# Attention scores and value products in one 64-row by 32-column tiling of the TensorE array, side results in the score slots

## The chip, the cores and the metric

One core of one Trainium2 chip runs the whole kernel. The metric is the device time of one execution in microseconds (us). Engines are named as in the profile: PE (TensorE, matmuls) and PEld (its weight loads), DVE (VectorE), ACT (ScalarE), POOL (GpSimd), SP (SyncE, which issues the DMAs). PSUM, where matmuls put their results, is used as eight banks of 128 partitions by 512 fp32 values, numbered 0 to 7.

## The reference

A block of three residual steps on x of 4096 tokens by 256 features. In short:

```python
x = x + 0.5 * ffn(layernorm(x))          # base 256x256, a shared and six routed rank-16 adapters, top 2 of 6
x = x + attn(layernorm(x))
x = x + 0.5 * ffn(layernorm(x))          # the same weights

def attn(x):                              # 16 heads of 16 features, T = 4096
    q, k, v = x @ Wq.T, x @ Wk.T, x @ Wv.T
    q, k = layernorm_per_head(q) * 256**-0.25, layernorm_per_head(k) * 256**-0.25
    dot = q @ k.T                         # per head, causal: j > i masked
    return (softmax(dot) @ v).reshape(T, 256) @ Wo.T + bo
```

## The kernel before

**Tiling.** Tokens are cut into 8 chunks of 512 queries (`CH`), heads into 4 groups of 4. For each chunk and group the keys are walked in blocks of 128. The work is counted in *units* (`attention_units`): a unit is 1024 columns of scores, two banks of PSUM, in full blocks two heads by 512 queries against one key block. Two units make a *batch* (one key block, four heads; one of the diagonal batches is a single unit). Chunk c has 20 + 32c units, 1056 in all, so chunks 1 to 7 have 52, 84, 116, 148, 180, 212 and 244.

**Stages of a unit.** `scores(u)` (L1356): for each of two heads a matmul of keys (50 rows: two fp16 parts of the head, their cross terms and two rows of shift; 128 key columns) by queries (512 columns, fp16), the two heads in the upper and lower 64 rows of the array and in the two banks of slot `u % 3` (`SLOTS = 3`: banks 0 to 5). `exp` (L776) on ACT reads the two banks at once, 1024 columns, and writes one of five places of the ring of probabilities (fp32). `mask` (L724) on POOL zeroes what lies above the diagonal. `values(b)` (L1374) takes a batch: for each of four heads a matmul of the 128 keys' values (17 columns: 16 features and a column of ones, which gives the softmax's sum) by the probabilities (128 rows, 512 columns, fp32), the four heads in four column strips of 32 and all in bank 6 (`ACC`). An fp32 matmul shows as two MATMUL records, so a full batch has eight. After a group's last batch DVE transposes bank 6 into SBUF (`gather`, L1159) and divides by the sum (`divide`, L1164, L1166).

**Side work.** Everything else (layernorms, the two FFNs of other chunks, q/k/v of the next chunk, the output projection of the one before) is cut into stages that are mixed into the attention of each chunk: `turn`, `turnin` and `heads` (four fp32 transposes each on PE), `qk` (6 matmuls of 512 columns), `value` and `projout` (12 of 256), `inner` (24 of 118), `outer` (18 of 256). Each such piece writes one bank, number 7 (`SIDE`), while attention runs, and DVE (for some stages of the first chunks ACT) reads it out. `turn` and `turnin` are read twice: a copy to fp16 (L846) and the remainder (L848).

**Order.** All engines follow one list, `ORDER` (`schedule`, L230). In step u it has: `exp` u, `mask` u, side stages of place 3u, `scores` u+2, `divide` where due, side stages of place 3u+1, `values` of a batch that ended at unit u-1 (u-2 if masked), side stages of place 3u+2. The table `PLACES` gives the place of each side stage within its chunk. Each engine executes its part of the list strictly in this order, waiting on semaphores. `Pass.__init__` walks the list once to find, for each stage that writes a side bank, which bank it gets and whom it must wait for (`bank`, `last`, `done`). Scores of unit u wait for `exp` of u-3, values for `exp` (or `mask`) of the batch's last unit.

Of the kernel before, what the change touches and what calls it, by code (L numbers as in the profile page):

```python
# [41 lines left out]
ACC, SIDE = 6, 7  # L42
START_BANKS = (7, 5, 4, 3)
END_BANKS = (7, 0, 1, 2, 3, 4, 5)
# [176 lines left out]
def schedule():  # L221
# [28 lines left out]
    for u in range(NU):  # L250
# [8 lines left out]
        if BATCHES[b][2][-1] == u:  # L259
            values.append((u + (2 if BATCHES[b][3] else 1), b))  # L260
# [13 lines left out]
    for _, b in values:  # L274
        yield "values", b
        if b in GROUP_END:
            yield "gather", GROUP_END[b]
            groups.append((NU, GROUP_END[b]))
# [55 lines left out]
class Pass:  # L334
# [5 lines left out]
    def __init__(self, name, semaphore, order, banks, scalar, x, x_in, fronts, free=None):  # L340
# [16 lines left out]
        self.use, self.bank, self.done, self.last, self.scalar, self.high = {}, {}, {}, {}, scalar, {}  # L357
        held, count, rotate = {}, {self.read: 0, self.read_act: 0}, True
        for stage, n in order:
            rotate = rotate and stage != "scores"  # L360
            if free and (stage, n) == ("exp", NU - 1):

                rotate, banks = True, END_BANKS
                held.update({b: free for b in END_BANKS if b != SIDE})
# [16 lines left out]
def build(nc, ap, out, always_general=False):  # L381
    ctx = ExitStack()
    with ctx:
# [93 lines left out]
        def bank(b, n=1):  # L477
# [14 lines left out]
        s_ok, exp_ok, mask_ok, pv, acc_read, bo_ok, att_ok = (semaphore(q) for q in (  # L492
            "s_ok", "exp_ok", "mask_ok", "pv", "acc_read", "bo_ok", "att_ok"))
# [8 lines left out]
        main = Pass("m", semaphore, ORDER, START_BANKS, on_scalar, x_main, lambda c: (x_in[c], 16), 2, (exp_ok, NU))  # L502
# [226 lines left out]
        def _(act):  # L729
# [25 lines left out]
            for stage, n in ORDER:  # L755
# [15 lines left out]
                elif stage == "exp":  # L771
# [4 lines left out]
                    act.activation(probs[:, u % RING, :], bank(2 * (u % SLOTS), 2), ACTF.Exp, bias=0.0, scale=1.0).then_inc(exp_ok, 1)  # L776

        @block.vector
        def _(dve):
# [324 lines left out]
            dve.memset(bank(ACC), 0.0).then_inc(zeroed, 1)  # L1104
# [44 lines left out]
            for stage, n in ORDER:  # L1149
                front_and_heads(main, stage, n)  # L1150
                if stage == "gather":
# [7 lines left out]
                    dve.transpose(oT[:, :], bank(ACC)).then_inc(acc_read, 1)  # L1159
                elif stage == "divide":  # L1160
# [5 lines left out]
                    dve.tensor_tensor(att[:, g // 2, :, g % 2 * HS:(g % 2 + 1) * HS], turned[:, :, 0:HS],  # L1166
# [282 lines left out]
```

## Time and profile before

| | |
|---|---|
| runs shown | 1196.37, 1195.91, 1195.37 us; median 1195.91 |
| span of the profiled execution | 1192.3 us, 3.6 us below that median (start and end of the program lie outside it) |
| PE busy | 1104.1 us, 93% |
| ACT busy | 1014.7 us, 85% |
| DVE, POOL busy | 467.5 and 241.6 us, 39% and 20% |
| first and last `exp` | about 96 and 1159 us from the start of the span |
| chain that ended last | PE 72%, ACT 13%, issue 6%, DVE 6% |

The page's busy time of PE is from the first column sent to the end of the last matmul as modelled; matmuls overlap, in different strips of the array above all, so a busy PE is not one at its peak. A timeline row gives the start of a group of like instructions, the time from its first start to its last end, their number, and in brackets how long the engine had been idle.

### The profile page before, as it was taken

To read this page: it belongs to the slowest core of one execution; us is meant where nothing else is said; L and a number is where in the kernel's file an instruction comes from. 1 tells how busy PE (TensorE), PEld (TensorE's weight loads), DVE (VectorE), ACT (ScalarE), POOL (GpSimd) and SP (SyncE) were. 2 spreads that over 40 slices of the span, in tenths; PEclk is the share of its full clock that TensorE was granted. 3 is DMA by queue.
4 is the path that set the end of the run, shared out by engine and by line. 5 is a ranking of instruction groups with operands and counts; after the bars stand their busy time and mean duration, and the time that the engine had idled before them with its cause. 6 is when DMAs were issued, how large, how long until landed. Compare 5 with 4: busy or idle time off the path is not lost.

```text
span 1192.3 us, 22761 instructions
## 1 busy us (share of the span) xinstructions
PE 1104.1 (93%) x8884; PEld 359.6 (30%) x8884; DVE 467.5 (39%) x1181; ACT 1014.7 (85%) x1134; POOL 241.6 (20%) x377
## 2 busy tenths in 40 slices
PE   3758999999999999999999999999999999999994
PEld 3534333332323233232332232232222222222123
DVE  5678665554544353333333323423131222021114
ACT  3216788789888998999999999999999999999980
POOL 2236533222122211212022021012110101010100
PEclk9779999999999999999999999999999999999996
DMA  5022202003000300003000022000001100000000
GB/s 145 3 63 60 59 11 81 1 28 99 1 1 19 93 17 1 1 32 92 4 1 1 1 67 60 1 1 2 1 10 48 53 1 1 10 10 1 1 19 18
DMA packets 39608, 33.37 MB, mean 28 GB/s; under 512 B 8722, under 2 KB 39432, under 8 KB 39496
## 3 DMA queue, kind: packets, MB, share of 16 engines
q1 hardware_dynamic: 37364, 31.74, 9.0%
q8 instruction: 73, 1.20, 0.4%
q10 hardware_dynamic: 2132, 0.12, 0.1%
q14 instruction: 39, 0.32, 0.1%
HBM read 18.73 MB, written 12.85 MB: 26 GB/s over the span
## 4 chain that ended last, share of the span: by engine, by line
PE 72%; ACT 13%; issue 6%; DVE 6%; DMA 1%; POOL 1%; SPq 0%; ACTq 0%; DVEq 0%; POOLq 0%
PE ps L1190 68%; ACT ring L776 13%; PE ps L1232 2%; PE ps L1298 1%; DMA x<-in_x 1%; DVE st L807 1%; PE ps L1252 1%; DVE area L828 1%; DVE oT L1159 0%; POOL rstd L711 0%; POOL sq L532 0%; DVE x L980 0%; DVE ss L985 0%; DVE sq L1013 0%; ACT area L765 0%
## 5 line engine op out<-in xcount | busy, mean ns | idle before, releaser
L776 ACT ACTIVATE ring<-ps 128x1024 f32<-128x1024 f32 x1056 | 982.2, 1115 | 65.5 <-PE ps L1190 63.5
L1190 PE MATMUL ps<-ring,vf 128*17 128x512 f32 (+3 forms) x4608 | 559.4, 562 | 5.0 <-DVE oT L1159 4.4
L1190 PE MATMUL ps<-queries,keys 50*128 50x512 f16 (+3 forms) x2304 | 363.2, 366 | 22.1 <-ACT ring L776 4.9
L1190 PEld LDWEIGHTS ps<-queries,keys 50*128 50x128 f16 x2304 | 92.3, 93 | 475.3 <-ACT ring L776 437.3
L724 POOL TENSOR_SCALAR_AFFINE_SELECT ring<-ring 128x256 f32<-128x256 f32 (+1 forms) x224 | 103.9, 481 | 396.5 <-ACT ring L776 392.6
L1190 PEld LDWEIGHTS ps<-ring,vf 128*17 128x17 f32 x4608 | 79.7, 95 | 174.5 <-issue 144.2
L711 POOL TENSOR_TENSOR rstd<-var,minus_half 128x4 f32<-128x4 f32 x24 | 24.4, 1017 | 235.6 <-DVE var L813 235.4
L980 DVE SCALAR_TENSOR_TENSOR x<-ps,power,x 128x512 f32<-128x512 f32 x32 | 24.0, 750 | 110.7 <-PE ps L1190 110.7
L846 DVE CAST xnT<-ps 128x512 f16<-128x512 f32 x32 | 22.1, 691 | 100.0 <-PE ps L1232 100.0
L1190 PE MATMUL ps<-baseT,xnT 128*128 128x256 f16 x384 | 55.0, 283 | 3.9 <-DVE area L848 3.8
L1232 PE MATMUL ps<-ident,area 128*128 128x128 f32 x192 | 34.2, 311 | 20.0 <-DVE area L828 20.0
L765 ACT ACTIVATE xnT<-ps 128x512 f16<-128x512 f32 x16 | 9.6, 599 | 49.9 <-PE ps L1232 49.9
L1159 DVE STREAM_TRANSPOSE oT<-ps 128x512 f32<-128x512 f32 x32 | 22.9, 715 | 71.0 <-PE ps L1190 70.5
L1190 PE MATMUL ps<-qkT,xnT 128*128 128x512 f16 x192 | 48.7, 394 | 1.7 <-DVE xnT L848 1.5
L532 POOL TENSOR_TENSOR sq<-area 128x512 f32<-128x512 f32 x32 | 33.5, 1047 | 67.2 <-DVE ss L985 41.7
L1190 PEld LDWEIGHTS ps<-baseT,xnT 128*128 128x128 f16 x384 | 36.7, 101 | 19.2 <-issue 11.0
L828 DVE TENSOR_SCALAR area<-x,mv,rstd 128x256 f32<-128x256 f32 x96 | 36.9, 444 | 11.3 <-POOL rstd L711 11.3
L1013 DVE TENSOR_SCALAR sq<-ps,scaled 128x512 f32<-128x512 f32 x16 | 12.9, 806 | 70.1 <-PE ps L1298 70.1
L537 POOL TENSOR_TENSOR split<-sq,split 128x512 f16<-128x512 f32 x16 | 18.8, 1175 | 100.0 <-DVE split L1017 100.0
L807 DVE BATCH_NORM_STATS2 st<-x 128x6 f32<-128x256 f32 x96 | 33.5, 412 | 9.5 <-DMA x<-in_x 4.8
L1232 PEld LDWEIGHTS ps<-ident,area 128*128 128x128 f32 x192 | 23.6, 156 | 43.0 <-issue 36.9
L848 DVE TENSOR_TENSOR xnT<-ps,xnT 128x512 f16<-128x512 f32 x48 | 33.1, 691 | 7.6 <-ACT xnT L765 6.3
(153 smaller groups left out, 670.5 us busy)
## 6 DMA issues: line engine op xcount, KB each, us to landing
parts_d<-split SPq DMA_DIRECT2D x32, 256.0 KB, 2.6
keys<-parts_d SPq DMA_DIRECT2D x96, 64.0 KB, 2.3
queries<-parts_d SPq DMA_DIRECT2D x192, 32.0 KB
x<-in_x SPq DMA_DIRECT2D x8, 512.0 KB, 4.2
out_x<-x SPq DMA_DIRECT2D x16, 256.0 KB, 2.2
queries<-shift_d SPq DMA_DIRECT2D x64, 4.0 KB
ring<-in_base_W SPq DMA_DIRECT2D x1, 256.0 KB, 4.9
ring<-in_Wq SPq DMA_DIRECT2D x1, 256.0 KB, 3.8
```

Of the source, the lines that this page charges most:

```text
L532: e.tensor_tensor(sq[:, :], qn[:, n % TC, :], qn[:, n % TC, :], ALU.mult).then_inc(K.sq_ok, 1)
L711: pool.tensor_tensor(rstd[ln][:, :], var[ln][:, 0, :], minus_half[:, :].broadcast_to([P, TC]), ALU.pow).then_inc(main.rstd_ok[ln], 1)
L724: m = pool.affine_select(out=tiles[:, part, :], in_=tiles[:, part, :], compare_op=ALU.is_ge, fill=0.0, base=0, pattern=[[0, len(range(8)[p ...
L776: act.activation(probs[:, u % RING, :], bank(2 * (u % SLOTS), 2), ACTF.Exp, bias=0.0, scale=1.0).then_inc(exp_ok, 1)
L807: dve.bn_stats(st[ln][:, i, :], x[:, i, :]).then_inc(*own.up())
L828: m = dve.tensor_scalar(xn[ln][:, i, :], x[:, i, :], mv[ln][:, i, 0:1], rstd[ln][:, i:i + 1], ALU.subtract, ALU.mult)
L846: dve.tensor_copy(high, src).then_inc(*K.own.up())
L848: dve.tensor_tensor(low, src, high, ALU.subtract).then_inc(K.read, 1)
L980: dve.scalar_tensor_tensor(out=x, in0=bank(K.bank[key]).rearrange("p (n d) -> p n d", n=2), scalar=power[0][:, 5:6], in1=x, op0=ALU.mult, ...
L1159: dve.transpose(oT[:, :], bank(ACC)).then_inc(acc_read, 1)
L1190: return pe.matmul(o, lhsT, rhs, start=start, stop=stop, skip_group_check=True)
L1232: m = pe.transpose(b[:, ib * D + i * P:ib * D + (i + 1) * P], xn[ln][:, 2 * a + i, ib * P:(ib + 1) * P], ident[:, :])
```

## The change

Three things, all in one diff.

1. **One tiling.** A score matmul of 50x128 keys becomes four of 50x32 (32 keys each), so a unit is 8 matmuls of 512 columns in the 8 tiles of 64 rows by 32 columns. A value matmul is cut by rows: 64 keys each, upper and lower half. The accumulator is now two banks, 6 and 7 (`ACC`), one for the even and one for the odd 128-query tiles of the chunk. A batch's values come in two parts. In part 0 the upper rows work on one bank and the lower rows on the other; in part 1 they swap. Each part of a full batch is 8 matmuls of 256 columns (16 MATMUL records). Part 1 waits for the semaphore `pv_first` that part 0 raises.
2. **Order.** Part 0 stands in the step of the batch's last unit (one step earlier than the values before), part 1 in the next step.
3. **Side results.** Bank 7 is gone as a side bank. A side piece takes a bank of one of the three score slots: the planner in `Pass.__init__` gives it the slot that comes free first, counts the slot as taken for `SIDE_UNITS` = 2.2 units, and lets a second piece within a step share it. Scores take the slot that comes free first, and wait for whoever used it, an `exp` or a side reader. `gather` transposes two banks of 256 columns, `divide` has two multiplications.

```diff
-ACC, SIDE = 6, 7
+ACC = 6, 7
+SIDE = 7
...
+SIDE_UNITS = 2.2
...
-            values.append((u + (2 if BATCHES[b][3] else 1), b))
+            values += [(u + (2 if BATCHES[b][3] else 0) + part, (b, part)) for part in range(2)]
...
-        while values and values[0][0] <= u:
-            b = values.pop(0)[1]
-            yield "values", b
-            if b in GROUP_END:
+        first = False
+        while values and values[0][0] <= u and not first:
+            b, part = values.pop(0)[1]
+            first = part == 0
+            yield "values", (b, part)
+            if part == 1 and b in GROUP_END:
...
+            elif stage == "scores":
+                s = min(range(SLOTS), key=lambda q: (free[q], q))
+                free[s], shared[s] = n + 1, -2
+                self.slot[n], self.slot_free[n] = s, sorted({held[b] for b in (2 * s, 2 * s + 1) if b in held}, key=lambda q: (q[0].name, q[1]))
+                held[2 * s] = held[2 * s + 1] = (exp_ok, n + 1)
             if stage in BANK_STAGES:
                 i = len(self.use)
-                b = banks[i % len(banks)] if rotate else SIDE
+                if rotate:
+                    b = banks[i % len(banks)]
+                else:
+                    s = min(range(SLOTS), key=lambda q: (shared[q] < now - 1, free[q], q))
+                    b = 2 * s + (last_side + 1) % 2 if shared[s] >= now - 1 else 2 * s
+                    free[s], shared[s], last_side = now + SIDE_UNITS, now, b
...
-                    act.activation(probs[:, u % RING, :], bank(2 * (u % SLOTS), 2), ACTF.Exp, bias=0.0, scale=1.0).then_inc(exp_ok, 1)
+                    act.activation(probs[:, u % RING, :], bank(2 * main.slot[u], 2), ACTF.Exp, bias=0.0, scale=1.0).then_inc(exp_ok, 1)
...
-                    dve.transpose(oT[:, :], bank(ACC)).then_inc(acc_read, 1)
+                    for i in range(2):
+                        m = dve.transpose(oT[:, i * CH // 2:(i + 1) * CH // 2], bank(ACC[i])[:, 0:CH // 2])
+                    m.then_inc(acc_read, 1)
...
-                if u >= SLOTS:
-                    pe.wait_ge(exp_ok, u - SLOTS + 1)
+                for key in main.slot_free[u]:
+                    pe.wait_ge(*key)
...
+                for pair in zip(blocks[0::2], blocks[1::2]):
+                    for k in range(0, P, 32):
+                        for h, j, q0, w, b, col in pair:
+                            half = slice(HR * (h % 2), HR * (h % 2) + SH + 2)
+                            m = mm(bank(2 * main.slot[u] + b)[k:k + 32, col:col + w], keys[half, h // 2, j * P + k:j * P + k + 32],
+                                   queries[half, h // 2, q0:q0 + w], True, True)
...
+                    pe.wait_ge(pv_first, b + 1)
+                runs = [], []
+                for h, j, q0, w, bk, col, u in [block + (u,) for u in units for block in UNITS[u][2]]:
+                    for rows in range(2):
+                        i = (b + part + rows) % 2
+                        tiles = [q for q in range(q0 // P, (q0 + w) // P) if q % 2 == i]
...
+                            runs[rows].append((h % GH, bank(ACC[i])[32 * (h % GH):32 * (h % GH) + VL, tiles[0] // 2 * P:(tiles[-1] // 2 + 1) * P],
+                                               vf[HALF * rows:HALF * (rows + 1), j, HEAD[h], :], moving))
+                for pair in itertools.zip_longest(*(sorted(runs[rows], key=lambda q: q[0]) for rows in range(2))):
+                    for run in pair:
+                        if run:
+                            m = mm(*run[1:], first and part == 0, last and part == 1)
+                m.then_inc((pv_first, pv)[part], 1)
```

How PE's instructions move, at a `turn` in chunk 6 (a piece of four transposes, `ps<-ident,area`). `ps<-queries,keys` are scores, `ps<-ring,vf` are values; the semaphores waited for stand in brackets (`m_read` is raised by DVE's reads of side banks, `exp_ok` by ACT's exponentials). PE before:

```order
L1190 MATMUL ps<-queries,keys 128x512 [waits exp_ok]
L1190 MATMUL ps<-queries,keys 128x512
L1232 MATMUL ps<-ident,area 128x128 [waits m_xn_ok0,const,m_read]
L1232 MATMUL ps<-ident,area 128x128 x3
L1190 MATMUL ps<-queries,keys 128x512 [waits exp_ok]
L1190 MATMUL ps<-queries,keys 128x512
L1190 MATMUL ps<-ring,vf 17x512 [waits exp_ok]
L1190 MATMUL ps<-ring,vf 17x512 x3
L1190 MATMUL ps<-queries,keys 128x512 [waits exp_ok]
L1190 MATMUL ps<-queries,keys 128x512
```

The same piece on PE after the change (L1214 and L1256 are the helpers L1190 and L1232):

```order
L1214 MATMUL ps<-ring,vf 17x256 [waits exp_ok]
L1214 MATMUL ps<-ring,vf 17x256 x7
L1256 MATMUL ps<-ident,area 128x128 [waits m_xn_ok0,const,exp_ok]
L1256 MATMUL ps<-ident,area 128x128 x3
L1214 MATMUL ps<-queries,keys 32x512 [waits exp_ok]
L1214 MATMUL ps<-queries,keys 32x512 x7
L1214 MATMUL ps<-ring,vf 17x256 [waits pv_first]
L1214 MATMUL ps<-ring,vf 17x256 x7
L1214 MATMUL ps<-queries,keys 32x512 [waits m_read,exp_ok]
L1214 MATMUL ps<-queries,keys 32x512 x7
```

The piece now waits for an exponential instead of the last reader of bank 7, the first values stand ahead of the next scores instead of behind them, and the second scores behind the piece wait for DVE's reads of it.

## Rows read from the trace of the kernel before

**Rows 1.** The page: busy time by engine; chain that ended last.
```profile
PE 1104.1 (93%) x8884; PEld 359.6 (30%) x8884; DVE 467.5 (39%) x1181; ACT 1014.7 (85%) x1134; POOL 241.6 (20%) x377
PE 72%; ACT 13%; issue 6%; DVE 6%; DMA 1%; POOL 1%; SPq 0%; ACTq 0%; DVEq 0%; POOLq 0%
```

**Rows 2.** Busy time by stretch, chunks 2, 3, 6, 7; length, engines, PEclk (granted clock), DMA.
```profile
190.00:282.00 92.00, 90.82 (x770) 30.72 (x762) 47.69 (x108) 78.84 (x86) 26.90 (x41) 1.00 0.14 42
282.00:404.00 122.00, 120.50 (x1012) 39.02 (x1008) 59.40 (x146) 108.69 (x119) 29.85 (x45) 1.00 0.10 28
...
727.00:930.00 203.00, 199.26 (x1590) 54.52 (x1586) 59.50 (x144) 197.08 (x216) 28.61 (x43) 1.00 0.04 13
930.00:1159.00 229.00, 218.31 (x1706) 54.21 (x1702) 38.14 (x96) 224.82 (x247) 18.98 (x35) 1.00 0.04 10
```

**Rows 3.** Chain of waits, 950 to 970 us, in order of time: start, length, what.
```profile
950.47 1.09 ACT ring L776
951.55 0.05 issue
951.60 8.16 PE ps L1190 x62
```

**Rows 4.** Timeline, 950 to 952 us: start, length, engine, instruction.
```profile
950.09 0.13 PEld L1190 LDWEIGHTS ps<-ring,vf 128*17 128x17 f32 x8 [0.23 <-issue]
950.09 1.05 PE L1190 MATMUL ps<-ring,vf 128*17 128x512 f32 x8
951.07 0.92 PE L1190 MATMUL ps<-queries,keys 50*128 50x512 f16 x4
```

**Rows 5.** Timeline, 839 to 843 us: a `qk` piece and what follows.
```profile
839.14 1.47 PE L1190 MATMUL ps<-qkT,xnT 128*128 128x512 f16 x6
840.54 0.39 PE L1190 MATMUL ps<-queries,keys 50*128 50x512 f16 x2
840.86 1.05 PE L1190 MATMUL ps<-ring,vf 128*17 128x512 f32 x8
841.85 0.61 PE L1190 MATMUL ps<-queries,keys 50*128 50x512 f16 x4
842.34 2.85 ACT L776 ACTIVATE ring<-ps 128x1024 f32<-128x1024 f32 x3 [0.28 <-PE ps L1190]
842.38 1.05 PE L1190 MATMUL ps<-ring,vf 128*17 128x512 f32 x8
```

**Rows 6.** Timeline of PE, 91 to 93.5 us, before attention begins.
```profile
91.22 0.60 PE L1232 MATMUL ps<-ident,area 128*128 128x128 f32 x4
91.66 1.46 PE L1190 MATMUL ps<-qkT,xnT 128*128 128x512 f16 x6
92.95 0.60 PE L1232 MATMUL ps<-ident,area 128*128 128x128 f32 x4
```

**Rows 7.** Timeline, 871 to 876 us: an `outer` piece.
```profile
871.53 0.83 PE L1190 MATMUL ps<-baseT,xnT 128*128 128x256 f16 x6
...
873.61 0.39 PE L1190 MATMUL ps<-queries,keys 50*128 50x512 f16 x2
...
874.10 1.02 ACT L776 ACTIVATE ring<-ps 128x1024 f32<-128x1024 f32 x1 [0.59 <-PE ps L1190]
```

**Rows 8.** Timeline, 751 to 757 us: a `turn` piece.
```profile
751.15 9.27 ACT L776 ACTIVATE ring<-ps 128x1024 f32<-128x1024 f32 x10
...
754.77 0.66 PE L1232 MATMUL ps<-ident,area 128*128 128x128 f32 x4
755.36 0.39 PE L1190 MATMUL ps<-queries,keys 50*128 50x512 f16 x2
755.46 0.69 DVE L846 CAST xnT<-ps 128x512 f16<-128x512 f32 x1 [4.79 <-PE ps L1232]
...
756.19 0.69 DVE L848 TENSOR_TENSOR xnT<-ps,xnT 128x512 f16<-128x512 f32 x1
```

**Rows 9.** Groups of instructions by line and shape: count, busy us, mean ns.
```profile
L776 ACT ACTIVATE ring<-ps 128x1024 f32<-128x1024 f32 x1056 | 982.2, 1115 | 65.5 <-PE ps L1190 63.5
...
L1190 PEld LDWEIGHTS ps<-ring,vf 128*17 128x17 f32 x4608 | 79.7, 95 | 174.5 <-issue 144.2
```

More of the change, by code:

```diff
@@ L273, in schedule @@
         yield from beside(3 * u + 2)
-    for _, b in values:
-        yield "values", b
-        if b in GROUP_END:
+    for _, (b, part) in values:
+        yield "values", (b, part)
+        if part == 1 and b in GROUP_END:
             yield "gather", GROUP_END[b]
@@ L334, with __init__ @@
 class Pass:
-    def __init__(self, name, semaphore, order, banks, scalar, x, x_in, fronts, free=None):
+    def __init__(self, name, semaphore, order, banks, scalar, x, x_in, fronts, exp_ok=None):
         def s(q):
@@ L1368, in scores @@
                         pe.wait_ge(main.k_in[c][g // 2], 6 * 16)
-                for h, j, q0, w, b, col in blocks:
-                    half = slice(HR * (h % 2), HR * (h % 2) + SH + 2)
-                    m = mm(bank(2 * (u % SLOTS) + b)[:, col:col + w], keys[half, h // 2, j * P:(j + 1) * P],
-                           queries[half, h // 2, q0:q0 + w], True, True)
+                for pair in zip(blocks[0::2], blocks[1::2]):
[4 more added lines that the diff above has]
+                                   queries[half, h // 2, q0:q0 + w], True, True)
@@ L1373, in scores, with values @@
                 m.then_inc(s_ok, 1)
-            def values(b):
+            def values(b, part):
                 c, g, units, masked, first, last = BATCHES[b]
-                if first and b >= 1:
-                    pe.wait_ge(acc_read, NG * c + g)
-                elif first:
-                    pe.wait_ge(zeroed, 1)
-                if first and g == 0:
-                    for a in range(2):
-                        pe.wait_ge(*main.done["value", (c, a)])
-                if masked:
-                    pe.wait_ge(mask_ok, MASKED[units[-1]])
-                else:
-                    pe.wait_ge(exp_ok, units[-1] + 1)
-                blocks = sorted([(q0, h % GH, h, j, w, u, bk, col) for u in units for h, j, q0, w, bk, col in UNITS[u][2]])
-                for q0, k, h, j, w, u, bk, col in blocks:
-                    m = mm(bank(ACC)[32 * k:32 * k + VL, q0:q0 + w], vf[:, j, HEAD[h], :], probs[:, u % RING, bk * CH + col:bk * CH + col + w], first, last)
-                m.then_inc(pv, 1)
@@ L1394, in _ @@
-            before = [q for q in ORDER[:ORDER.index(("scores", 0))] if q[0] in BANK_STAGES]
-            side_last = [main.done[[q for q in before if main.bank[q] == b][-1]] for b in START_BANKS[1:]]
+                if part == 0:
+                    if first and b >= 1:
+                        pe.wait_ge(acc_read, NG * c + g)
+                    elif first:
+                        pe.wait_ge(zeroed, 1)
+                        pe.wait_ge(*main.acc_free)
+                    if first and g == 0:
+                        for a in range(2):
+                            pe.wait_ge(*main.done["value", (c, a)])
+                    if masked:
+                        pe.wait_ge(mask_ok, MASKED[units[-1]])
+                    else:
+                        pe.wait_ge(exp_ok, units[-1] + 1)
+                else:
+                    pe.wait_ge(pv_first, b + 1)
@@ L1400, in _ @@
                 elif stage == "values":
-                    values(n)
+                    values(*n)
                 elif stage == "projout":
```

39 lines of the change are left out of this document (26 added, 13 removed).

## The prediction

> **What bounds the kernel now.** I read the page first, then the stretches, then single timelines. On the page PE is the busiest engine and the chain that ended last lies on it for 72%, on ACT for 13% [rows 1]. The stretches say that this is no one bound. A run of undisturbed `exp` (ten in 9.27 us, the last lasting 1.115) starts one every (9.27 - 1.115) / 9 = 0.906 us [rows 8, 9]. By that pace the units of chunks 2, 3, 6 and 7 would take 76.1, 105.1, 192.1 and 221.1 us. Their stretches took 92, 122, 203 and 229 [rows 2]. ACT therefore lost 15.9, 16.9, 10.9 and 7.9 us there: ACT is the floor, and PE sometimes comes late. About 1063 us of the span are attention, against 1056 x 0.906 = 957 for the exponentials alone.
>
> **What PE pays for a change of tiling.** Six `qk` matmuls take 1.29 us where four fp32 transposes of the same 128x128 tiling follow (91.66 to 92.95), and the transposes 0.44 each time [rows 6]; going from fp32 to fp16 costs nothing. Where scores follow, the same six take 839.14 to 840.54, 1.40 us [rows 5]. The number format is the same there and the tiling changes: 0.11 us a switch. Scores to values and back cost that too: values take 0.99 us (840.86 to 841.85), two units of scores 0.53 (841.85 to 842.38) [rows 5], a batch 1.52. Without the two switches it is 1.30: scores 0.21 a unit, values 0.44 a half. The Trainium skill (TensorEngine Tiling (Array Packing), Key Properties) says that changing the tiling mode drains TensorE; by that rule, the trace agrees.
>
> **The time PE has.** An `exp` starts 0.49 us after the first matmul of its scores when ACT is waiting (873.61 to 874.10, 841.85 to 842.34) [rows 5, 7]. PE continues 0.05 after an `exp` has ended [rows 3], that is 1.16 after its start. So scores released by the `exp` three units back have 3 x 0.906 - 1.16 - 0.49 = 1.07 us until ACT stalls. Let time 0 be PE's release by the last `exp` of a batch, step E; the step after it is O.
>
> Before: O's scores start at 0, values 0.32 to 1.31, the next E's scores at 1.31 (limit 0.906 + 1.07 = 1.98), PE idle from 1.63 to 1.81. A side piece may be 0.67 long without a stall if it stands behind O's scores, or at place 0 of E, and 0.85 if it stands in front of O's scores, using the idle 0.18. I test this on the trace. Long pieces last, with their switch, 1.40 (`qk`), 2.08 (`outer`, 871.53 to 873.61 [rows 7]), and by 0.11 a matmul of 256 columns about 1.42 (`value`, `projout`) and 1.32 (`inner`), 22.2 us in a full chunk. In chunk 6, 13 of its 14 have 0.85 and one 0.67: 22.2 - 11.7 = 10.5 against 10.9 found. In chunk 7 eight have 0.85: 13.8 - 6.8 = 7.0 against 7.9. Chunks 2 and 3 give 9.2 and 12.5 against 15.9 and 16.9: there pieces stand 4 units apart and PE does not recover between them (chunk 3: 58 x 1.52 + 29.3 of side pieces = 117 of 122 us).
>
> **After, term by term.** The order is now: values part 0 at 0 to 0.44, O's scores at 0.44 (limit 1.07), part 1 to 1.09, next E's scores at 1.09 (limit 1.98), idle from 1.30 to 1.81. The idle time grows from 0.18 to 0.51, but:
> - A piece now pays two switches, one more (0.11), and eight tiles start one after another. Eight weight loads of 0.095 fit in 0.13 [rows 4, 9], some 0.005 apart, so I take 0.04 for the last of eight.
> - A piece at place 1 asks for the slot of the running `exp` and waits for its end: it can't use the idle time. Behind it come a half of values, then scores. It has 1.07 - 0.44 = 0.63 (E), 1.98 - 0.906 - 0.44 = 0.63 (O).
> - At place 2 of E or place 0 of O it has 0.63, at place 2 of O or place 0 of E 1.98 - 1.09 = 0.89.
>
> Less 0.15 for the first point, the room is 0.48 or 0.74. Counted in the order, 90 long pieces: 36 go from 0.85 to 0.48 (+0.37 each), 17 from 0.67 to 0.48 (+0.19), 37 from 0.67 to 0.74 (-0.07): 13.3 + 3.2 - 2.6 = **+13.9 us**. Short pieces last 0.59 (754.77 to 755.36 [rows 8]) and stall nothing now; 32 of them will be 0.11 over: **+3**.
>
> Then the side readers. Bank 7 made nobody wait but the next side piece; now 140 units of scores wait for a reader, usually four units after the piece. A `turn` is read out 2.11 after its start (754.77 to 756.19 + 0.69) [rows 8], 2.2 with release and switch, against a limit of 1.98 after its slot was released. At place 1 (14 pieces read twice) that is 0.2 late, at place 2 of O (11, started 0.18 later) 0.4, of E (5, 0.44 later) 0.65: 10 us, less what is counted above, **+8.5** if DVE is free at once. Pieces at place 0 start a unit earlier and are in time; single reads of 0.7 behind long pieces stay inside the stall that the piece has made.
>
> What dense chunks get back: PE's need in chunk 3 falls from 117 to 58 x 1.30 + 29.3 + 26 x 0.11 = 107.6, some 4 more for part 1's wait on part 0 (0.07 each, when only one unit of scores lies between), against ACT's 105. The 4.4 and 6.7 us lost there beyond the single pieces (chunks 3, 2) should shrink by more than half, and chunks 0, 1 and 4 give some: **-10**, between 0 and -15. The tail: part 1 waits for part 0 with nothing between, two transposes for one, two multiplications: **+0.5**. `gather`, `divide` and the unbalanced parts of one diagonal batch in each group (32 x 0.2 us of PE) lie beside ACT otherwise.
>
> Sum: 13.9 + 3 + 8.5 - 10 + 0.5 = 15.9 on the span of 1192.3; with the 3.6 outside it, **1211 us**. PE's work falls by 528 x 0.22 - 167 x 0.11 = 98 us (167 side pieces, 90 long and 77 short), and the time does not follow, since ACT sets the pace and the slots are fewer.
>
> **The eight tiles.** No row shows fp32 in both row halves at once, and none eight tiles. Bounds: full overlap, as in the four strips [rows 4] and the two score halves, or a load that isn't hidden. In the trace eight loads run under the first four matmuls in the same rows (950.09), so I take full overlap. The Trainium skill (TensorE: Matmul & The Clock Gate, The mechanism) says that LDWEIGHTS overlaps in-flight matmuls only when the row group differs; here the trace disagrees. It is a rival below.
>
> **Rivals.**
> - *Faster: the relief of PE wins.* If rooms stay as they are (scores caught up by the 0.51 idle time, DVE quick), only the dense term is left: 1196 - 10 = 1186, at best some 1178. For: PE is on 72% of the chain. Against: the room counted above decides, not PE's sum; it turns where the mean room of long pieces exceeds today's 0.75. Chance 0.27.
> - *Nothing to measure:* terms cancel within 0.2%, 2.4 us, which is what a measurement here can tell. 0.08.
> - *Slower by my sum:* 1211 (1199 to 1222). 0.42.
> - *Readers are late.* DVE works in order and is busy a third to a half of the time [rows 2]; behind a read stand operations of 0.4 to 0.8 us or a wait for another engine, and scores, hence ACT, wait for it. Another 0.2 at each of 140 units: about +25, 1236. 0.16.
> - *Loads or row halves don't overlap.* If each wave of eight (six in a batch) pays a load of 0.095, a batch is 1.87 and everything is bound by PE: 528 x 1.87 and about 90 x 1.6 + 77 x 0.59 of side pieces make 1177 in place of 1063, 1310 us. It decides from 0.5 us more a batch. 0.07.
>
> **Numbers.** The likeliest is 1211. The range 1186 to 1236 takes in the bounds of the dense and the reader's term and half of the faster case. Faster 0.27, same 0.08, slower 0.65.
>
> **What would show it.** Right: no step of 0.1 between scores and values, a batch's matmuls 1.3 apart where PE is behind, PE idle more, and more than 11 and 8 us lost by ACT in chunks 6 and 7, less than 16 and 17 in chunks 2 and 3. Scores four units behind a `turn` would be released by DVE's second read of it. Wrong: stalls behind single long pieces in chunk 6 no longer than now (the rooms were miscounted); a gap left at scores to values (the switch was not the tiling); or starts of eight matmuls spread by more than 0.1 us (the tiles don't overlap).

## The result and the profile after

The changed kernel takes 1309.4 us (median of 4 runs, 1307.11 to 1312.3), beside 1196.03 for the kernel before on the same chip: ratio 1.095, 95% interval 1.0932 to 1.0969. It is slower by 113 us. The forecast had the sign, 15 us and a range that ended at 1236. One rival names 1310 us; it met the number by chance, since what it says of the hardware is not what the traces below show.

The page of the changed kernel, the rows that answer to [rows 1] and the first of [rows 9]:

```profile
PE 1125.3 (86%) x29108; PEld 558.9 (43%) x29108; DVE 480.6 (37%) x1245; ACT 1024.6 (78%) x1134; POOL 237.3 (18%) x377
...
PE 42%; ACT 24%; issue 19%; DVE 11%; DMA 1%; SPq 1%; POOL 1%; DVEq 0%; ACTq 0%; POOLq 0%
...
L794 ACT ACTIVATE ring<-ps 128x1024 f32<-128x1024 f32 x1056 | 991.7, 1066 | 159.8 <-PE ps L1214 156.0
```

One `exp` lasts less than before (1066 ns against 1115), yet ACT is idle 160 us in front of its exponentials where it was 65.5. PE's share of the last chain falls from 72% to 42%, and DVE's rises from 6% to 11%: more of the time is waiting from engine to engine. The same four stretches as [rows 2], chunks 2, 3, 6 and 7:

```profile
217.00:324.00 107.00, 95.44 (x2447) 48.02 (x2442) 48.76 (x117) 80.16 (x86) 27.14 (x41) 0.98 0.12 35
324.00:459.00 135.00, 122.72 (x3264) 62.35 (x3256) 63.13 (x153) 109.91 (x120) 29.25 (x45) 1.00 0.10 27
810.00:1031.00 221.00, 200.41 (x5564) 92.02 (x5544) 60.33 (x152) 199.30 (x216) 28.27 (x43) 1.00 0.06 15
1031.00:1271.00 240.00, 217.69 (x6256) 94.09 (x6240) 39.51 (x104) 226.02 (x247) 17.95 (x35) 1.00 0.05 13
```

Against the pace of 0.906 us a unit, ACT now loses 30.9, 29.9, 28.9 and 18.9 us there, where it lost 15.9, 16.9, 10.9 and 7.9. Nothing came back in the dense chunks.

**Does the tiling work?** A plain stretch of the changed kernel's timeline in chunk 6:

```profile
1000.02 0.66 PE L1214 MATMUL ps<-ring,vf 64*17 64x256 f32 x16 [0.16 <-ACT ring L794]
1000.25 0.14 PEld L1214 LDWEIGHTS ps<-queries,keys 50*32 50x32 f16 x8
1000.46 0.43 PE L1214 MATMUL ps<-queries,keys 50*32 50x512 f16 x8
1000.80 0.16 PEld L1214 LDWEIGHTS ps<-ring,vf 64*17 64x17 f32 x16 [0.40 <-PE ps L1214]
1000.80 0.65 PE L1214 MATMUL ps<-ring,vf 64*17 64x256 f32 x16
1001.24 0.43 PE L1214 MATMUL ps<-queries,keys 50*32 50x512 f16 x8
1001.86 0.65 PE L1214 MATMUL ps<-ring,vf 64*17 64x256 f32 x16 [0.18 <-ACT ring L794]
```

It does. A part (16 records) holds PE for 0.44 us, from 1000.02 to 1000.46, as forecast for a half without switches; the next scores follow at once, and their eight weights were loaded 0.2 us earlier under running matmuls. The next batch begins 1.84 later, about ACT's pace for two units (1.81), and PE waits for ACT there. The one flaw is small: part 1 starts 0.78 after part 0 and not 0.66, as it waits for part 0's last matmul to end.

**Where ACT loses time.** For the other comparisons I counted over each trace how much later than 0.906 us after the last one each `exp` starts. *Start of a group* means a masked unit or one of the four behind it, *full* everything else; delays under 0.03 are left out. *Scores*: the `exp` starts within 0.16 us of its scores' end. *Ring*: its scores were ready and it waited for something else. That is the place in the ring, or another instruction of ACT's own just ahead of it (a read of a side result, or the router's): at group starts 15 of the 31 us before are of the second kind and 16 of the 111 after, so the ring proper went from 16 to 95.

| us lost, all chunks | full, scores | full, ring | start, scores | start, ring | sum |
|---|---|---|---|---|---|
| before | 49 | 3 | 22 | 31 | 106 |
| after | 75 | 10 | 24 | 111 | 220 |

So 33 of the 114 us are in full stretches, and 81 at the starts of groups, a place to which the prediction gave no time of ACT's, only some of PE's.

**A bare start of a group**, with no side piece near it (first units 600 and 601, chunk 6, changed kernel, timeline):

```profile
813.08 4.14 ACT L794 ACTIVATE ring<-ps 128x1024 f32<-128x1024 f32 x4
...
814.31 0.41 PE L1214 MATMUL ps<-queries,keys 50*32 50x512 f16 x8
814.53 0.62 PE L1214 MATMUL ps<-ring,vf 64*17 64x256 f32 x16
815.23 0.41 PE L1214 MATMUL ps<-queries,keys 50*32 50x512 f16 x8
...
817.57 1.02 ACT L794 ACTIVATE ring<-ps 128x1024 f32<-128x1024 f32 x1 [0.35 <-PE ps L1214]
```

The ring has five places: `exp` u waits on `pv` until *all* values of the batch of unit u-5 are done (`pv` is raised by part 1 alone). Part 1 of units 600 and 601 starts at 814.53 and ends at 815.15; `exp` 605, whose scores were ready, starts at 815.28, 0.40 us late (the four exponentials from 813.08 take 4.14 us, at the pace 3 x 0.906 + 1.07 = 3.79). `exp` 607 at 817.57 is 0.46 late in the same way. Masked values stood two steps after their batch before the change; now part 0 stands there and part 1 a step later still. This start costs 0.87 us; it cost 0.03.

**The same place with a side piece**, units 706 to 711 of the changed kernel, timeline:

```profile
924.12 1.47 PE L1214 MATMUL ps<-qkT,xnT 128*128 128x512 f16 x6 [0.29 <-ACT ring L794]
...
925.52 0.41 PE L1214 MATMUL ps<-queries,keys 50*32 50x256 f16 x16
...
926.16 0.24 DVE L1184 RECIPROCAL den<-oT 128x16 f32<-128x16 f32 x1
926.43 0.64 DVE L1189 TENSOR_TENSOR att<-oT,den 128x128 f32<-128x128 f32 x2
927.00 0.68 DVE L854 COPY area<-ps 128x512 f32<-128x512 f32 x1
...
927.83 0.41 PE L1214 MATMUL ps<-queries,keys 50*32 50x512 f16 x8 [1.89 <-DVE area L854]
928.04 0.63 PE L1214 MATMUL ps<-ring,vf 64*17 64x256 f32 x16
...
929.56 1.94 ACT L794 ACTIVATE ring<-ps 128x1024 f32<-128x1024 f32 x2 [2.47 <-PE ps L1214]
```

The `qk` result is complete at 925.6, but DVE still has the router's work, the division and then the copy: it is read out at 927.68. The second scores behind the piece want that slot, so PE stands for 1.89 us, with the overdue values queued behind it, and ACT is idle for 2.47 us: first without scores (until 928.2), then without a place in the ring (until the values end at 929.47). This start loses 3.53 us, against 0.35 before.

Two theories stand against each other for the 98 us that the forecast missed. **Ring**: masked values a step later use up the five places. **Readers**: scores wait for DVE's read of a side bank. A third, **tiling**, would have the half batches and their order themselves cost more than they free.

### The profile page after: what moved, and what is told of

It reads as the page before. It is cut to its first block, busy times and chain, and to the rows that moved or that the text cites. A ratio compares the mean times of both kernels' runs of the same rounds, so it can differ in the third digit from the quotient of the medians.

```text
span 1305.4 us, 63412 instructions
## 1 busy us (share of the span) xinstructions
PE 1125.3 (86%) x29108; PEld 558.9 (43%) x29108; DVE 480.6 (37%) x1245; ACT 1024.6 (78%) x1134; POOL 237.3 (18%) x377
## 4 chain that ended last, share of the span: by engine, by line
PE 42%; ACT 24%; issue 19%; DVE 11%; DMA 1%; SPq 1%; POOL 1%; DVEq 0%; ACTq 0%; POOLq 0%
PE ps L1214 39%; ACT ring L794 24%; PE ps L1256 2%; DVE st L825 1%; DMA x<-in_x 1%; PE ps L1322 1%; DVE area L846 1%; DVE oT L1178 1%; DVE xnT L866 1%; DVE x L998 1%; DVE xnT L864 1%; SPq L616 1%; DVE att L1189 1%; SPq L604 1%; PE ps L1276 0%
## 5 line engine op out<-in xcount | busy, mean ns | idle before, releaser
L794 ACT ACTIVATE ring<-ps 128x1024 f32<-128x1024 f32 x1056 | 991.7, 1066 | 159.8 <-PE ps L1214 156.0
L1214 PE MATMUL ps<-ring,vf 64*17 64x256 f32 (+1 forms) x17920 | 696.4, 369 | 36.1 <-ACT ring L794 27.2
L1214 PE MATMUL ps<-queries,keys 50*32 50x512 f16 (+2 forms) x9216 | 448.5, 363 | 81.0 <-ACT ring L794 47.4
L1214 PEld LDWEIGHTS ps<-ring,vf 64*17 64x17 f32 x17920 | 240.0, 93 | 331.6 <-ACT ring L794 140.4
L1214 PEld LDWEIGHTS ps<-queries,keys 50*32 50x32 f16 x9216 | 150.7, 92 | 246.0 <-ACT ring L794 137.5
L742 POOL TENSOR_SCALAR_AFFINE_SELECT ring<-ring 128x256 f32<-128x256 f32 (+1 forms) x224 | 99.8, 461 | 434.1 <-ACT ring L794 431.3
L1214 PE MATMUL ps<-baseT,xnT 128*128 128x256 f16 x384 | 56.8, 289 | 4.8 <-DVE area L866 3.6
L1178 DVE STREAM_TRANSPOSE oT<-ps 128x256 f32<-128x256 f32 x64 | 24.9, 427 | 75.1 <-PE ps L1214 74.5
L1256 PE MATMUL ps<-ident,area 128*128 128x128 f32 x192 | 34.7, 315 | 20.2 <-DVE area L846 19.7
L1214 PE MATMUL ps<-qkT,xnT 128*128 128x512 f16 x192 | 48.5, 393 | 2.2 <-DVE xnT L866 1.5
L1214 PEld LDWEIGHTS ps<-baseT,xnT 128*128 128x128 f16 x384 | 37.3, 103 | 20.5 <-issue 8.7
L1256 PEld LDWEIGHTS ps<-ident,area 128*128 128x128 f32 x192 | 23.9, 157 | 37.9 <-issue 30.0
L854 DVE COPY area<-ps 128x512 f32<-128x512 f32 x20 | 13.8, 688 | 67.8 <-PE ps L1214 67.7
L825 DVE BATCH_NORM_STATS2 st<-x 128x6 f32<-128x256 f32 x96 | 33.5, 412 | 11.5 <-DMA x<-in_x 7.0
```

The costliest lines, as they stand in the source:

```text
L742: m = pool.affine_select(out=tiles[:, part, :], in_=tiles[:, part, :], compare_op=ALU.is_ge, fill=0.0, base=0, pattern=[[0, len(range(8)[p ...
L794: act.activation(probs[:, u % RING, :], bank(2 * main.slot[u], 2), ACTF.Exp, bias=0.0, scale=1.0).then_inc(exp_ok, 1)
L825: dve.bn_stats(st[ln][:, i, :], x[:, i, :]).then_inc(*own.up())
L1178: m = dve.transpose(oT[:, i * CH // 2:(i + 1) * CH // 2], bank(ACC[i])[:, 0:CH // 2])
L1214: return pe.matmul(o, lhsT, rhs, start=start, stop=stop, skip_group_check=True)
L1256: m = pe.transpose(b[:, ib * D + i * P:ib * D + (i + 1) * P], xn[ln][:, 2 * a + i, ib * P:(ib + 1) * P], ident[:, :])
```

## The experiments

In each, the ratio is to the kernel before on the same chip (its medians were 1193.6 to 1195.2). "From after" and "from before" say which kernel was edited.

### One cause at a time

**a_mask1**, from after: masked values one step earlier.

```diff
-            values += [(u + (2 if BATCHES[b][3] else 0) + part, (b, part)) for part in range(2)]
+            values += [(u + (1 if BATCHES[b][3] else 0) + part, (b, part)) for part in range(2)]
```

> The changed kernel, with both parts of a masked batch's values one step earlier (the second part where all of it stood before the change). Theory 'ring': exp u waits for the values of u-5 in the five-place ring, and the second part came one step later than the values did, so at the 28 diagonal group starts of chunks 1 to 7 exp stands waiting for values. Then the time falls from 1309 to 1235 to 1285 us, and the two stalls of 0.4 us in a bare group start (units 605 and 607) go. Rival 'slots': the stalls at group starts come from scores and side pieces that wait for a slot's reader, with the values queued behind them; then under 10 us come back. The earlier part may wait up to 0.5 us on POOL's mask, behind nothing that ACT needs at once.

1274.62 us, 1.0665 (1.0641 to 1.069): 35 us of the 113 come back by one digit. At the same bare start of a group ACT now runs through unit 605; 607 is still 0.48 us late, where the expectation had both stalls gone:

```profile
788.72 3.93 ACT L794 ACTIVATE ring<-ps 128x1024 f32<-128x1024 f32 x4
...
790.78 0.60 PE L1214 MATMUL ps<-ring,vf 64*17 64x256 f32 x13 [0.42 <-POOL ring L742]
...
792.81 2.85 ACT L794 ACTIVATE ring<-ps 128x1024 f32<-128x1024 f32 x3 [0.17 <-PE ps L1214]
```

Part 0 of units 602 and 603 now waits 0.42 us for POOL's mask, and part 1, for which `exp` 607 waits, stands behind it: the earlier place has a price too. The loss by the ring at group starts falls from 111 to 69 us (the ring proper from 95 to 42); by scores it rises from 24 to 32.

**a_order**, from after: both parts where the values stood before the change.

```diff
-            values += [(u + (2 if BATCHES[b][3] else 0) + part, (b, part)) for part in range(2)]
+            values += [(u + (2 if BATCHES[b][3] else 1), (b, part)) for part in range(2)]
-        while values and values[0][0] <= u and not first:
+        while values and values[0][0] <= u:
```

> The changed kernel, with both parts of a batch's values together in the step where the values stood before. Theory 'ring': the second part is again as early as before in masked batches, so the group starts lose 25 to 60 us less; in full batches part 1 waits about 0.3 us for part 0 with nothing between, the next scores start at 1.42 instead of 1.09 us and long pieces have some 0.4 instead of 0.48 us of room: 5 to 10 us more. In sum 1250 to 1290. Rival 'slots': no gain at group starts, 1310 to 1325.

1350.5 us, 1.1317 (1.1287 to 1.1348), above what either theory allowed and, with a_two below, the slowest here. Group starts lose 125 us, 10 less than in the changed kernel, but full stretches 133 instead of 85. The timeline shows why:

```profile
1000.57 0.64 PE L1212 MATMUL ps<-queries,keys 50*32 50x512 f16 x16
1001.00 1.42 PE L1212 MATMUL ps<-ring,vf 64*17 64x256 f32 x32
1002.22 0.64 PE L1212 MATMUL ps<-queries,keys 50*32 50x512 f16 x16
```

A batch takes 1.65 us, against 1.52 before: with nothing between the parts, values hold PE 1.22 (1001.00 to 1002.22) and not 0.88. Part 1 waits for part 0, and those 0.34 us are more than the two switches (0.22) cost. Splitting the batch over two steps is no ornament: the tiling needs it.

**b_slots**, from before: tiling and order untouched, side results put in score slots by the change's planner; bank 7 stays empty.

```diff
-                b = banks[i % len(banks)] if rotate else SIDE
+                else:
+                    s = min(range(SLOTS), key=lambda q: (shared[q] < now - 1, free[q], q))
+                    b = 2 * s + (last_side + 1) % 2 if shared[s] >= now - 1 else 2 * s
+                    free[s], shared[s], last_side = now + SIDE_UNITS, now, b
```

> The kernel before in its old tiling and order, with side results in the three score slots by the planner of the change (bank 7 idle in attention). By the rooms of the prediction: 36 long pieces from 0.85 to 0.67 (+6.5 us), 17 behind O's scores from 0.67 to 0.08, since they wait for the running exp (+10), readers late +10 to +20: 1220 to 1235. If slots cost nothing by themselves: 1196. If they are the whole loss: near 1309.

1277.97 us, 1.0696 (1.0675 to 1.0717), in none of the three forecasts: the slots cost 83 us by themselves, on average half a microsecond for each of 167 pieces. A `turn` of this kernel, timeline:

```profile
882.03 0.66 PE L1246 MATMUL ps<-ident,area 128*128 128x128 f32 x4
882.61 0.39 PE L1204 MATMUL ps<-queries,keys 50*128 50x512 f16 x2
882.72 0.69 DVE L860 CAST xnT<-ps 128x512 f16<-128x512 f32 x1 [6.29 <-PE ps L1246]
883.44 0.69 DVE L862 TENSOR_TENSOR xnT<-ps,xnT 128x512 f16<-128x512 f32 x1
884.28 0.39 PE L1204 MATMUL ps<-queries,keys 50*128 50x512 f16 x2 [1.28 <-DVE xnT L862]
...
884.77 1.02 ACT L790 ACTIVATE ring<-ps 128x1024 f32<-128x1024 f32 x1 [0.43 <-PE ps L1204]
```

Scores start 2.25 us after the start of the piece, right after DVE's second read, though DVE was free at once; `exp` is 0.43 late. The length of that wait was forecast (2.2), how often it counts was not. The longest of PE's waits from 100 to 1150 us in this kernel (in all, times, longest):

```profile
PE ps L1204 <- ACT ring L790: 32.8, 62, 1.6
PE ps L1204 <- DVE xnT L862: 13.2, 18, 1.3
PE ps L1204 <- DVE x L994: 6.0, 8, 1.7
PE ps L1204 <- DVE area L850: 5.7, 5, 1.9
PE ps L1204 <- DVE area L862: 4.2, 5, 1.3
PE ps L1204 <- DVE x L1198: 3.3, 5, 0.7
```

and the same list of the kernel before, where only two waits of 0.4 and 0.2 us in all follow:

```profile
PE ps L1190 <- ACT ring L776: 4.9, 12, 0.5
PE ps L1190 <- DVE oT L1159: 4.4, 3, 3.1
PE ps L1298 <- DVE area L1002: 1.6, 1, 1.6
```

Readers of side results are hardly in the second; in the first the five groups of them cost PE 32 us. PE's waits for `exp` grow by nearly as much (4.9 to 32.8): while a piece has a slot, scores must take one that a later `exp` still holds. The wait for readers and the wait for `exp` are both prices of sharing. This run doesn't separate them; a_side3 below trades one for the other.

**b_ring4**, from before: one place of the ring fewer, memory as it was.

```diff
-RING = 5
+RING = 4
```

> The kernel before with a ring of four places of probabilities in use instead of five. Theory 'ring': the ring is the limit at masked batches; with four places exp n of the first unit behind a masked batch comes 0.75 us late, twice or three times at each of 28 group starts, and full batches lose their slack behind pieces: 1250 to 1300, with ACT's waits at group starts. Rival: values are never what ACT waits for, under 1205.

1260.41 us, 1.0548 (1.0527 to 1.057). Time lost by the ring goes from 34 to 151 us, by scores from 72 to 20. The ring had no place to spare before the change; a step of delay is not free anywhere. (Six places weren't tried.)

### Which pieces pay for the slots

Three kernels from b_slots give bank 7 back to one class of pieces each, b_slots_g, b_slots_t and b_slots_l in this order. The condition stands ahead of the planner's choice:

```diff
+                elif any(UNITS[v][3] is not None for v in range(max(0, now - 2), min(NU, now + 3))):
+                elif stage in SPLIT_STAGES:
+                elif stage in ('qk', 'value', 'projout', 'inner0', 'inner1', 'outer0', 'outer1'):
+                    b = SIDE
```

> b_slots (1278 us), but the 55 side pieces that stand within two steps of a masked unit use bank 7 as before the change. Theory 'group starts': in b_slots exp lost 91 us there against 53 before, so 30 to 45 of the 83 us come back: 1233 to 1248. Rival 'everywhere alike': 55 of 167 pieces, 27 us: 1248 to 1255.

> b_slots, but the 49 pieces that DVE reads twice (turn, turnin) use bank 7. Theory 'readers': a turn alone in a full stretch costs 0.3 to 1.0 us in b_slots and nothing before, long pieces only 0.0 to 0.6 more than before: 49 x 0.65 = 32 us come back, 1240 to 1252. Rival 'running exp': the pieces' own wait for the running exp and the scores that wait two exps back are what costs, whatever the reader: 49 of 167, 24 us, 1252 to 1258.

> b_slots, but the 90 long pieces use bank 7; only the 77 short ones are in slots. Theory 'readers': shorts carry most of the cost: 18 to 30 us come back, 1248 to 1260. Rival 'running exp': long pieces carry it, since they can't use PE's idle time: 50 us or more come back, under 1230.

| bank 7 has | us | ratio (95%) | gained on b_slots | per piece |
|---|---|---|---|---|
| 55 near masked units | 1244.07 | 1.0422 (1.0396 to 1.0448) | 34 | 0.62 |
| 49 read twice | 1245.83 | 1.0425 (1.0397 to 1.0454) | 32 | 0.66 |
| 90 long | 1237.01 | 1.0351 (1.0325 to 1.0376) | 41 | 0.45 |

The first two came out as the theory in front had it, the third between its theory and its rival. No class is innocent. The first also says where group starts lose: with bank 7 there, the ring's loss at group starts is 33 us, beside 59 in b_slots and 31 before. With the long ones in bank 7, the 77 short ones still cost 43 us, 0.56 each. The forecast had 11.5 us for the short ones (3 and 8.5), and for the long ones their smaller rooms but nothing for their reader.

**a_side3**, from after: the planner counts a slot as taken a unit longer, so that scores come to it later.

```diff
-SIDE_UNITS = 2.2
+SIDE_UNITS = 3.2
```

> The changed kernel with the planner counting a slot as taken by a side piece for 3.2 units instead of 2.2: 355 instead of 226 units of scores wait for the exp two back, and readers have a unit more. Theory 'readers late are the cost': 20 us or more come back, under 1290. Theory 'the lost room is the cost' (scores with 0.16 us): 1310 to 1330.

1289.25 us, 1.0794 (1.0773 to 1.0815), 20 us better. By the order, 143 units of scores wait for a reader, as in the changed kernel, but further behind the piece; the price is that 355 instead of 226 scores must wait for the `exp` two units back. From 100 to 1150 us PE's waits for readers of side results fall from some 27 to 7 us (those for L866 from 6.0 us in 11 waits to 0.2 in one). The ring's loss at group starts hardly moves, 107 us for 111: what comes back lies in full stretches (85 to 70 us) and, at 7 us, at group starts.

### What the tiling itself does

Two score slots instead of three, and a fixed bank for side results that nobody else uses: no reader can hold scores up, and PE has little room, so its work should show.

```diff
-SLOTS = 3
+SLOTS = 2
```

That is all of **b_two** (from before, side bank 7). **a_two** (from after) has side results in bank 5 as well, **a_two_mask1** has a_mask1's line on top, and **a_two_alt** uses banks 4 and 5 in turn.

> The kernel before with two score slots (banks 0 to 3) and bank 7 for side results, banks 4 and 5 idle. Scores now wait for the exp two back and have 0.16 us until ACT stalls. A batch's values (0.99 us in one piece, two switches) then hold the next scores back by 0.25 us: 528 x 0.25 = 132 us and more behind pieces, 1330 to 1400.

> The changed kernel's tiling and order with two score slots (banks 0 to 3) and one bank, 5, for side results. Theory 'relief is real': with values in halves of 0.44 us and no switches each scores unit still comes within its 0.16 us, a plain batch keeps ACT's pace of 1.81 us, and pieces pay for a room of 0.27: 1250 to 1300, 60 us or more under b_two. Theory 'tiling gives nothing': like b_two within 20 us.

> a_two with the masked values one step earlier. Theory 'ring': again 25 to 40 us under a_two. If it comes under 1275 (a_mask1), taking side results out of the score slots is worth more than the third slot.

> a_two_mask1 with two banks for side results, 4 and 5 in turn. If pieces that follow closely wait for the one bank's reader in the dense chunks 1 to 4, 5 to 15 us come back: 1267 to 1277. If the bank is free again by the time the next piece comes, 1279 to 1284.

| | us | ratio (95%) | lost: full | lost: group starts |
|---|---|---|---|---|
| b_two | 1339.93 | 1.1217 (1.1199 to 1.1236) | 134 | 113 |
| a_two | 1349.1 | 1.1315 (1.1279 to 1.1351) | 98 | 161 |
| a_two_mask1 | 1281.69 | 1.0731 (1.0707 to 1.0755) | 91 | 102 |
| a_two_alt | 1279.51 | 1.0727 (1.0682 to 1.0773) | 91 | 101 |

With the masked values mended, tiling and order together gain 58 us on b_two, most of it in full stretches (134 to 91; a_two, 98, has most of that as well, although as a whole it came out as its theory 'tiling gives nothing' had it). Left as the change has them, the late masked values eat all of that: a_two is the slower of the two. The relief of PE is therefore real where slots are scarce, and the third theory falls for that case. With three shared slots the two effects cancel: against b_slots, a_mask1 loses 11 us less in full stretches (88 to 99) and 10 more at group starts (101 to 91). Three slots, two accumulator banks and a side bank of its own make nine banks, and there are eight, so the tiling alone can't be run. A second side bank gives nothing (2 us, intervals overlap). The change's own trade, three slots shared, is worth 7 us against two slots and a fixed bank (1274.62 to 1281.69, each with the early mask).

### Moving the side pieces

If the rooms of the prediction are right, pieces moved to the roomier places should gain. **a_seat** leaves place 0 of E and puts everything else at place 2 of O; **b_seat** leaves place 0 of O and puts the rest behind E's scores. Here are a_seat's function and, under it, b_seat's:

```diff
+def seat(place):
+    u, r = divmod(place, 3)
+    last = BATCHES[BATCH_OF[u]][2][-1] == u
+    if last and r and u + 1 < NU and BATCHES[BATCH_OF[u + 1]][2][-1] != u + 1:
+        return 3 * (u + 1) + 2
+    return place if last else 3 * u + 2
...
+def seat(place):
+    u, r = divmod(place, 3)
+    last = BATCHES[BATCH_OF[u]][2][-1] == u
+    if last:
+        return 3 * u + max(r, 1)
+    return place if r == 0 else 3 * (u + 1) + 1
```

> The changed kernel with side stages moved only within a batch: everything not at place 0 of E goes to place 2 of O, the two seats with 0.74 instead of 0.48 us of room by the prediction. Theory 'rooms': 53 long pieces gain 0.26 us each, 13.8 us: 1290 to 1300 against 1309. Rival: the seat doesn't matter, what counts is that a slot is taken at all, so within 4 us of 1309.

> The kernel before with side stages moved within a batch to the seats with 0.85 us of room (behind E's scores; place 0 of O stays). Theory 'rooms': 54 long pieces gain 0.18 us each, 9.7 us: 1184 to 1190. Rival: seats don't matter, 1193 to 1198.

Both are slower: a_seat 1330.96, 1.1132 (1.1113 to 1.1151), 22 us worse than after; b_seat 1222.76, 1.0232 (1.0215 to 1.0249). Neither theory had room for that, in either kernel. In b_seat chunks 5 to 7 lose 14.2, 10.5 and 8.8 us, as before or 2 more, and chunks 0 to 4 together 27 more. Where pieces are sparse the room rule costs or gives little; where they stand close, moving each by itself brings two together. That is a reading of the count by chunk; I made no run that shows the meeting of two pieces as the cause.

**a_away** and **b_away** add: from chunk 2 on, no side piece from one step ahead of a group to four behind (they go to step 8, at place 1 in b_away). The pieces of a chunk keep their order, so those behind a moved piece wait for it. a_away has the early mask too.

```diff
+        if first - 1 <= u <= first + 7 and place < 3 * (first + 8):
+            if u <= first + 4:
+                return 3 * (first + 8) + 0
```

> The changed kernel with masked values one step earlier (1275 us), the seats of a_seat, and from chunk 2 on no side stage in the steps -1 to 4 around a group's start (they move to step 8). Theory 'group starts': there a side piece holds back scores (slot, reader behind gather and divide on DVE), the masked values queue behind them and the ring of five makes exp wait; without pieces there about half of the 101 us that are lost at group starts come back: 1215 to 1240. Rival: the loss at group starts is that of the masks and of uneven value parts themselves, and moves with the pieces or stays: 1255 to 1270.

> The kernel before with the seats of b_seat and no side stage in the steps -1 to 4 around a group's start from chunk 2 on. Theory: 53 us are lost at group starts, with pieces there; 10 to 25 us come back beyond b_seat: 1162 to 1180. Rival: pieces collect at step 8 and stall there instead: 1184 to 1196.

1323.72, 1.1073 (1.1054 to 1.1091), and 1264.11, 1.0574 (1.0556 to 1.0592), both slower than either side of their expectation. The group starts do get better (b_away 47 us lost there, b_seat 72), but full stretches lose twice as much (131 against 63), probably where the pieces now stand together at step 8; no run shows that.

### A version that beats both?

**b_mask1**, from before: masked values at u+1, as all others. **a_best**, from after: a_mask1's and a_side3's lines together.

```diff
-            values.append((u + (2 if BATCHES[b][3] else 1), b))
+            values.append((u + 1, b))
```

> The kernel before with the values of masked batches one step earlier. Theory 'ring': 31 us of exp's waits at group starts end with values; some of them are the ring's: 1180 to 1192. Rival: PE then waits on POOL's masks, with scores behind: 1196 to 1215.

> The changed kernel with both mends: masked values one step earlier and 3.2 units for a slot with a side piece. If ring and readers are separate causes the gains add: 1309 - 35 - 20 = 1254 (1248 to 1262). If they are largely the same stalls (values queued behind scores that wait for a reader): 1265 to 1275.

b_mask1: 1208.54, 1.012 (1.0096 to 1.0143). One step earlier is worth 35 us after the change and costs 15 before it: the ring's loss at group starts falls from 31 to 26 (the ring proper from 16 to 2, ACT's own work in front of an `exp` rises from 15 to 25), but by scores 42 are lost instead of 22, as PE, with scores behind it, now waits for masks (5.2 us on L724, none before) and longer for `gather` (8.7 against 4.4). a_best: 1250.41, 1.0463 (1.0438 to 1.0488), 59 us below after, so the two gains (35 and 20) add. No version found beats the kernel before. The longest waits of a_best on PE from 100 to 1150 us:

```profile
PE ps L1214 <- ACT ring L794: 40.6, 175, 1.5
PE ps L1214 <- DVE oT L1178: 13.9, 14, 3.5
PE ps L1214 <- POOL ring L742: 2.4, 5, 1.1
PE ps L1214 <- DVE x L1208: 2.2, 1, 2.2
PE ps L1214 <- DVE area L854: 1.4, 2, 0.8
```

What now leads behind ACT is `gather` (L1178): the next group's first values wait for the transposes of the accumulator.

## Why the prediction was right or wrong

- **The bound and the sign: right.** ACT sets the pace, and 98 us less work for PE did not shorten anything while slots and places limit how far PE may fall behind.
- **The tiles: right.** Full overlap was taken, and the timeline shows it: waves of eight start within about 0.05 us and a part lasts 0.44. The rival of loads that don't overlap gives a batch of 1.87 us bound by PE; in the plain stretch above PE waits for ACT before each batch (1000.02, 1001.86), and 83 us of the 113 appear with no change of tiling at all (b_slots). Its 1310 is a coincidence. The Trainium skill (TensorE: Matmul & The Clock Gate, The mechanism) has weight loads overlap only where the row group differs; here eight loads into rows in use run under the matmuls (1000.25 above), so the trace disagrees with that sentence again. The same section of the Trainium skill also lets a load come early into a background weight buffer, which would fit the trace; no run here tells.
- **"`gather`, `divide` and the unbalanced parts … lie beside ACT otherwise": wrong, and by place the largest miss (81 of the 114 us that ACT lost more).** That sentence covers the starts of groups with nothing but PE's sum. There values are late by two steps, part 1 by three, and the ring of five, which the prediction never priced, turns each delay into one of ACT. The diff showed it: `2 if BATCHES[b][3]` became a time for part 0, with `part` added. Measured: the ring proper takes 79 us more at group starts (16 to 95). One step's shift of the masked values takes 53 of them away, and 35 from the whole time, as PE then waits for masks and scores come later (67 from the whole time in the pair with two slots). Shared slots alone, in the old tiling, bring the ring proper to 35 (b_slots), and bank 7 for the pieces near masked units brings it back to 17 (b_slots_g). It is the sharing, and not only the reader's delay: a_side3 cut PE's waits for readers to a quarter and left the ring's loss nearly where it was (111 to 107), with more scores waiting for a later `exp` in exchange.
- **Side readers +8.5, "if DVE is free at once", and the rival of +25: mechanism right, size wrong, and by cause the larger miss.** Scores do wait for the second read, 2.25 us after the start of the piece as against 2.2 forecast. But slots alone cost 83 us, of which readers are one part and scores that find the other slots taken another. The prediction priced only pieces read twice, and by their lateness in an empty stretch. Short pieces cost 0.56 us each and long ones 0.45, and near a group's start DVE has the division and the router's work in front of the read (1.89 us of PE in the example).
- **Rooms, +13.9: about right, for single pieces.** Behind a lone 1.4 us piece in a full stretch the exponentials lose 0.79 (place 1 of E) and 1.09 (place 2 of E), forecast 0.92; before it was 0.55, forecast 0.55. The term is an eighth of the change in time. It was also read as a rule for moving pieces, and a_seat and b_seat show that it isn't one.
- **Dense chunks −10: wrong.** Chunks 2 and 3 lose 15 and 13 us more, not less. The relief exists (58 us with two slots and early masked values) but with shared slots other waits take its place: a_mask1 and b_slots are 3 us apart, with intervals that overlap.
- **Part 1's wait +0.07: 0.12 each**, as it waits for the end of the last matmul; without effect while ACT sets the pace.
- **Small slips in the working.** The sum gives 1211.8 us, not 1211. The order has 143 units of scores that wait for a reader, not 140. DVE is busy 52, 49, 29 and 17% of the stretches in [rows 2], not "a third to a half". None of them moves the forecast by more than 1 us.

The terms do not add: b_slots gives +83, and tiling with late masked values brings it to +113, tiling with early ones to +80.

## What to carry to other kernels

Before pricing a change by the busy time it moves, list every buffer with a fixed number of places between two engines (slots, ring, accumulator) and count for each the steps from its last write to its last read, at the *worst* place of the order (group starts, masked blocks), not in the plain stretch. A bank that is free most of the time is not spare: it keeps a slow reader from standing between two fast engines, and sharing it made 167 side results cost half a microsecond each on average, in this kernel. When a consumer is split into two parts, the buffer is held until the second.

## What the hardware showed

- Eight tiles of 64 rows by 32 columns run fp32 side by side: 16 records of 256 columns in 0.44 us up to the next start, their starts within 0.05 us for a wave.
- Scores in fp16 (50 rows) follow fp32 values in the same tiling with no step: at 1000.46 they start 0.22 us after the second wave of values, which started 0.23 after the first. In the kernel before, a switch between tilings cost 0.11 [rows 5, 6].
- A part that waits for the other one right ahead of it costs 0.34 us of PE: two parts of 0.44 us take 1.22 back to back (a_order).
- The granted clock of chunk 2's stretch is 0.98 here, 1.00 in [rows 2]. No run separates its effect.
